# A graph network in one kernel: the attention stage's run masks computed earlier, some of its steps on GpSimd, and its block work in another place

## What is computed

```python
h = x @ W
alpha = x_i @ wa[:c] + edge_attr @ wa[c:c + ce] + x_j @ wa[c + ce:]   # x_i = h[dst], x_j = h[src]
alpha = jnp.where(alpha > 0, alpha, NEG_SLOPE * alpha)
m = jax.ops.segment_max(alpha, dst, num_segments=n)
a = jnp.exp(alpha - m[dst])
s = jax.ops.segment_sum(a, dst, num_segments=n)
out = jax.ops.segment_sum(a[:, None] * x_j, dst, num_segments=n) / (s + 1e-16) + bias
```

## Time and profile before

| | |
|---|---|
| median of 3 runs | 3713.82 us (3712.94 to 3720.65) |
| the profiled execution | 3718.32 us, of which the core's span is 3716.5 us |
| busy over the span | PE 80%, DVE 79%, ACT 59%, POOL 38% |
| mean granted clock of TensorE | 0.929 |
| dense passes | about 1353 to 1840 us |
| edge layer | about 1840 to 2796 us |
| attention stage | about 2796 to 3716 us |

### The profile page before, as it was taken

How to read it: one execution, slowest core, us unless ns; L and a number is a source line. 1 busy time by engine, 2 the same in 40 slices (tenths; PEclk the granted TensorE clock), 3 DMA queues, 4 the chain that set the end, 5 groups by cost and what they waited for, 6 DMA issues and landing times.

```text
span 3716.5 us, 122116 instructions
## 1 busy us (share of the span) xinstructions
PE 2983.3 (80%) x50473; PEld 2682.6 (72%) x50473; DVE 2931.3 (79%) x4854; ACT 2185.8 (59%) x5807; POOL 1425.5 (38%) x1155
## 2 busy tenths in 40 slices
PE   0299999999999969999777877887776878887886
PEld 0177777777777759888777777877766877777775
DVE  7599999999999933323488888888857988999996
ACT  6333333333443330000298988898866888898887
POOL 2000000000000000000089988998983555565554
PEclk9989999999999989999899999999986898899887
DMA  8156666766766679898687877777847888888784
GB/s 221 57 154 208 211 215 211 217 211 213 218 216 215 215 279 370 340 346 324 222 299 263 271 239 255 265 258 252 271 148 262 280 271 263 279 278 271 266 280 133
DMA packets 606666, 907.43 MB, mean 244 GB/s; under 512 B 358505, under 2 KB 494858, under 8 KB 587163
## 3 DMA queue, kind: packets, MB, share of 16 engines
q1 hardware_dynamic: 583992, 800.62, 66.2%
q10 hardware_dynamic: 19763, 94.38, 6.8%
q0 software_dynamic: 2352, 4.52, 0.5%
HBM read 651.96 MB, written 247.40 MB: 242 GB/s over the span
## 4 chain that ended last, share of the span: by engine, by line
PE 35%; DVE 25%; ACT 16%; issue 9%; POOL 6%; DMA 6%; ACTq 2%; DVEq 0%; SPq 0%; POOLq 0%
PE ps L648 9%; PE ps L1013 7%; ACT U L1593 4%; DMA U<-AD 4%; PE ps L673 3%; ACT U L550 3%; POOL EDG L1234 3%; DVE U L800 3%; DVE EDG L1721 2%; DVE U L1773 2%; POOL EDG L1226 2%; ACT U L1295 2%; PE ps L660 2%; PE ps L633 2%; PE ps L630 2%
## 5 line engine op out<-in xcount | busy, mean ns | idle before, releaser
L550 ACT ACTIVATE U<-ps 128x512 bf16<-128x512 f32 (+1 forms) x637 | 345.5, 571 | 460.4 <-PE ps L660 454.1
L493 POOL DMA_INDIRECT U<-REC,nod x49 | 78.4, 1600 | 1096.6 <-PE ps L604 975.6
L1226 POOL TENSOR_TENSOR EDG<-U,edge 128x512 f32<-128x512 f32 (+1 forms) x196 | 213.1, 1092 | 730.9 <-DVE edge L1378 697.7
L1593 ACT ACTIVATE U<-U,T 128x65 f32<-128x65 f32 x1806 | 459.7, 340 | 31.4 <-PE ps L1684 28.6
L1013 PE MATMUL ps<-U 128*128 128x192 bf16 x4802 | 417.9, 247 | 31.8 <-DMA U<-AD 31.2
L1013 PEld LDWEIGHTS ps<-U 128*128 128x128 bf16 x4802 | 401.8, 98 | 41.4 <-DMA U<-AD 38.4
L820 DVE TENSOR_TENSOR EDG<-edge,EDG 128x1792 bf16<-128x1792 bf16 x343 | 371.6, 1084 | 46.3 <-issue 25.9
L673 PE MATMUL ps<-EDG,U 128*128 128x193 bf16 x2401 | 313.0, 254 | 88.3 <-ACT U L550 65.8
L1621 POOL TENSOR_TENSOR U<-U 128x455 f32<-128x455 f32 x258 | 285.8, 1109 | 233.2 <-DVE U L1773 233.2
L648 PE MATMUL ps<-U 128*128 128x98 bf16 (+1 forms) x5292 | 373.2, 234 | 0.0
L648 PEld LDWEIGHTS ps<-U 128*128 128x128 bf16 x5292 | 361.8, 104 | 5.4
(11 more groups left out here) (321 smaller groups left out, 6929.6 us busy)
## 6 DMA issues: line engine op xcount, KB each, us to landing
U<-ROWS SPq DMA_DIRECT2D x411, 448.0 KB, 4.6
U<-AD SPq DMA_DIRECT2D x98, 1568.0 KB, 8.7
OND<-EDG SPq DMA_DIRECT2D x343, 224.0 KB
OSD<-EDG SPq DMA_DIRECT2D x343, 224.0 KB
AD<-U ACTq DMA_DIRECT2D x49, 1568.0 KB
EDG<-ROWS SPq DMA_DIRECT2D x171, 448.0 KB, 6.2
U<-OND SPq DMA_DIRECT2D x303, 224.0 KB, 5.0
U<-OSD SPq DMA_DIRECT2D x213, 224.0 KB, 4.7
```

The costliest lines, as they stand in the source:

```text
L550: ev4.by(act.activation(prow[i % NPW][:, P * g:P * (g + m)], ps[4 + gg % 2][:, 0:P * m], ACT.Copy))
L1226: ins = pool.tensor_tensor(VD[:, v:v + w, 0, KA * D:G * D].rearrange("p w (k f) -> p w k f", f=D), W_, bc(c_.unsqueeze(3), [P, w, G - KA, ...
L1593: ins = act.activation(V4[k % NV][:, 0, c, :], H[k % NHR][:, c, :], ACT.Copy, scale=a4[d % 2][:, s:s + 1])
```

## The change

Three things change, all for the attention stage.

1. The run masks of all 49 blocks are computed by POOL while the dense passes run (`passes_pool`), seven blocks at a time, from one load of the target numbers (2401 pieces of 256 bytes). SP stores them to memory (MSK, bf16, in seven transfers during the second pass), and in the attention stage loads 49 x 512 bytes for each block (`run_masks`) into two small buffers. PE's transpose L1641, ACT's copy L1579 and POOL's four instructions are gone there.
2. Of seven steps g = 0..6, POOL makes the values of g = 3 (`GV`) in place of ACT, with one multiplication of 128x455, and the first remainders of g = 1 and 5 (`GR`) in place of DVE. `value_at` and `rest_at` pick the semaphore to wait for. (The order on POOL: value, first remainder, second remainder.)
3. On PE the block matmuls of offsets 8, 10 and 12 come after the spread of their iteration instead of before it. On DVE the exponents (offset 15) come ahead of the first remainder.

```diff
+        def passes_pool(pool):
...
+            pool.wait_ge(msk_ld.at, msk_ld.o + 16)
+            for g in range(NGB):
...
+                msk_d.by(pool.tensor_tensor(mdif[:, :, 1:P], mdst[:, bl, 1:P], mdst[:, bl, 0:P - 1], ALU.subtract))
+                pool.wait_ge(msk_d.at, msk_d.o + 4 * g + 3)
+                msk_d.by(pool.tensor_scalar(mdif, mdif, 0.0, 1.0, ALU.is_equal, ALU.subtract))
+                pool.wait_ge(msk_d.at, msk_d.o + 4 * g + 4)
+                msk_ok.by(pool.tensor_scalar(mboth[:, bl, 0, :], mdif[:, :, 0:P], BIG, None, ALU.mult))
+                msk_ok.by(pool.tensor_scalar(mboth[:, bl, 1, :], mdif[:, :, 1:P + 1], -1.0, None, ALU.mult))
+            pool.wait_ge(msk_st.at, msk_st.o + 16 * NGB)
+
         def passes_sp(sp):
+            msk_ld.by(sp.dma_start(mdst, ROWS3[1].rearrange("d (s r) -> s d r", r=P)), 16)
             for p in range(2):
                 for i in range(NB):
                     r = i % NA
+                    if p and i % GB == GB - 1:
+                        g = i // GB
+                        sp.wait_ge(msk_ok.at, msk_ok.o + 2 * g + 2)
+                        msk_st.by(sp.dma_start(MSK[GB * g:GB * g + GB].rearrange("d s m r -> s d (m r)"),
...
             sp.wait_ge(row_mm.at, 2 * NB)
+            sp.wait_ge(msk_st.at, msk_st.o + 16 * NGB)
...
+        GV, GR = (3,), (1, 5)
...
+            def run_masks(d):
+
+                if d >= 2:
+                    sp.wait_ge(ytr.at, ytr.o + d - 1)
+                mk_ld[d % 2].by(sp.dma_start(masks[d % 2], MSK[d]), 16)
+
             sp.wait_ge(att.at, NGB)
             nt = 0
+            run_masks(0)
+            run_masks(1)
...
                 d, g, k = due4(t, 16)
-                if k is not None:
+                if k is not None and g not in GV:
                     act.wait_ge(exo.at, exo.o + d + 1)
...
+                d, g, k = due4(t, 16)
+                if k is not None and g in GV:
+                    pool.wait_ge(exo.at, exo.o + d + 1)
+                    pool.wait_ge(zok.at, zok.o + d + 1)
+                    pool.wait_ge(hev.at, hev.o + k + 1)
+                    if k >= NV:
+                        pool.wait_ge(sprd.at, sprd.o + k - NV + 1)
+                    vop.by(pool.tensor_tensor(V4[k % NV][:, 0, :, :], H[k % NHR],
+                                              bc(a4[d % 2][:, G * g:G * g + G].unsqueeze(2), [P, G, 65]), ALU.mult))
+                d, g, k = due4(t, 17)
+                if k is not None and g in GR:
+                    value_at(pool, k)
+                    rop.by(pool.tensor_tensor(V4[k % NV][:, 1, :, :], V4[k % NV][:, 0, :, :], S4[k % NV][:, 0, :, :], ALU.subtract))
                 d, g, k = due4(t, 18)
                 if k is not None:
-                    pool.wait_ge(rok.at, rok.o + k + 1)
+                    rest_at(pool, k)
...
                 d, g, k = due4(t, 17)
-                if k is not None:
-                    dve.wait_ge(vok.at, vok.o + k + 1)
+                if k is not None and g not in GR:
+                    value_at(dve, k)
...
-                    dve.wait_ge(flg.at, flg.o + 2 * d + 2)
-                    dvf.by(dve.tensor_tensor_scan(ysc, negs, ps[2][0:NB, 0:P], -BIG, ALU.add, ALU.max))
+                    dve.wait_ge(mk_ld[d % 2].at, mk_ld[d % 2].o + 16 * (d // 2 + 1))
+                    dvf.by(dve.tensor_tensor_scan(ysc, masks[d % 2][:, 0, :], ps[2][0:NB, 0:P], -BIG, ALU.add, ALU.max))
```

More of the change, by code:

```diff
@@ L1462, in cell @@
             return rows[k // 2 % n][:, e:e + P]
-        seg, negs, lastf, ylast = (Tflat[0:NB, 1225 + 130 * n:1225 + 130 * n + w] for n, w in enumerate((129, P, P, P)))
+        ylast = Tflat[0:NB, 1615:1615 + P]
+        masks = [MISC[0:NB, 1365 + P * i:1365 + P * i + P].bitcast(BF16).rearrange("p (m r) -> p m r", m=2) for i in range(2)]
+        identh = ident[0:NB, 0:NB].bitcast(BF16).rearrange("p (r h) -> p r h", h=2)[:, :, 1]
         ysc = ps[3][0:NB, P:2 * P]
@@ L1499, in due4, with value_at, rest_at @@
             return (k // G, k % G, k) if 0 <= k < NT else (None, None, None)
+        GV, GR = (3,), (1, 5)
+        def value_at(eng, k):
+            d, g = k // G, k % G
+            if g in GV:
+                eng.wait_ge(vop.at, vop.o + d * len(GV) + GV.index(g) + 1)
+            else:
+                eng.wait_ge(vok.at, vok.o + d * (G - len(GV)) + sum(h not in GV for h in range(g + 1)))
+        def rest_at(eng, k):
+            d, g = k // G, k % G
+            if g in GR:
+                eng.wait_ge(rop.at, rop.o + d * len(GR) + GR.index(g) + 1)
+            else:
+                eng.wait_ge(rok.at, rok.o + d * (G - len(GR)) + sum(h not in GR for h in range(g + 1)))
         def block4(t, off):
@@ L1544, in pairs4_sp @@
                     hots(k)
+                d = block4(t, 2)
+                if d is not None and d >= 2:
+                    run_masks(d)
                 d = block4(t, 40)
@@ L1686, in pairs4_pe @@
                     sprd.by(ins)
+                d = block4(t, 8)
+                if d is not None:
+                    pe.wait_ge(zok.at, zok.o + d + 1)
+                    if d:
+                        pe.wait_ge(ylok.at, ylok.o + d)
+                    ztr.by(pe.transpose(ps[2][0:NB, 0:P], z4[d % 2], ident[:, :]))
+                d = block4(t, 10)
+                if d is not None:
+                    pe.wait_ge(ylok.at, ylok.o + d + 1)
+                    if d:
+                        pe.wait_ge(ysok.at, ysok.o + d)
+                    pe.transpose(ps[3][:, 0:NB], ylast, ident[0:NB, 0:NB])
+                    ytr.by(pe.matmul(ps[3][:, 64:64 + NB], masks[d % 2][:, 1, :], identh, start=True, stop=True))
+                d = block4(t, 12)
+                if d is not None:
+                    pe.wait_ge(ysok.at, ysok.o + d + 1)
+                    if d:
+                        pe.wait_ge(miok.at, miok.o + d)
+                    for s in range(NB):
+                        k = G * d + s // G
+                        if s % G == 0:
+                            pe.wait_ge(od_ld[k % 4].at, od_ld[k % 4].o + 16 * (k // 4 + 1))
+                        ins = pe.matmul(ps[4][:, 4 * s:4 * s + 4], ODn[k % NOD][:, s % G, :], Y4[:, s, :], start=True, stop=True)
+                    ymm.by(ins)
         def pairs4_dve(dve):
@@ L1828, in pairs4_dve @@
                     miok.by(dve.tensor_tensor(RIf[:, d, 5:6], rest, RI[:, d, 4:5], ALU.subtract))
-                d = block4(t, 15)
-                if d is not None:
-                    dve.wait_ge(alg.at, alg.o + d + 1)
-                    dvf.by(dve.tensor_reduce(g4, ps[5][:, 0:6 * NB].rearrange("p (i v s) -> p i v s", v=2, s=3), AX, ALU.add))
-                    own()
-                    dvf.by(dve.tensor_tensor(w4, z4[d % 2], g4[:, :, 0], ALU.add))
-                    own()
-                    dvf.by(dve.scalar_tensor_tensor(w4, w4, 0.2, w4, ALU.mult, ALU.max))
-                    own()
-                    exi.by(dve.tensor_tensor(a4[d % 2], w4, g4[:, :, 1], ALU.subtract))
                 d = block4(t, 26)
@@ L2397, in _ @@
             with pool.Else():
+                passes_pool(pool)
                 pairs3_pool(pool)
```

85 lines of the change are left out of this document (28 added, 57 removed).

## The result

The changed kernel takes 3726.56 us (median of 14 runs) against 3712.03 us before (median of 14). The ratio is 1.0037, with a 95% interval from 1.0026 to 1.0048: slower by 0.4%, on the other side of the forecast of 3673 us and outside its range.

The account below looks back on a forecast made before the run. VectorE, partly kept out by GpSimd, was taken as the bound: 12.5 own work, 2.5 standing, 0.6 gaps and 1.1 to 1.3 waits a block, 45 us less over 49 blocks, plus 4 in the dense passes: 3673 us, range 3615 to 3707.

Parts of the forecast that it names:

- What bounds the kernel: Attention stage: VectorE sets the pace at 17.77 us a block, 2.3 of it standing behind GpSimd at a shared SBUF port.
- Standing behind GpSimd: Attention stage: VectorE's time kept out by GpSimd instructions, 2.3 us a block before, taken as 2.5 after.
- The wait term: VectorE in the attention stage: waits of 1.1 to 1.3 us a block, beside 0.6 us of gaps.
- bursts: GpSimd running value and remainders back to back, 3.8 and 2.8 us a block, with VectorE perhaps stalled to each one's middle.
- Block work later: TensorE in the attention stage: the spread no longer stands behind the scan, which had 75.2 us of waits.
- The cross-check: Time VectorE or GpSimd may use what they share: 15.9 us a block (89.5%) before, 15.45 (92% of 16.84) after.
- The port rival: VectorE and GpSimd's shared port stays the bound in the attention stage: block 17.26 us, 3693 us in all; chance 0.17.
- The slower rival: VectorE meets both GpSimd runs in their middle, standing 4.3 us a block instead of 2.3: 3752 us; chance 0.11.
- signs of being right: Scans 16.8 us apart, no 2.77 us L1721, its mean 0.85 to 0.95, no exp wait over 20, first AD 3 to 4 later.
- signs of being wrong: VectorE remainders at 1.5 us, index-load waits beyond 40 us, unchanged VectorE plus GpSimd time and period, or TensorE waiting for AD throughout.
- Dense passes: Start of the first pass: the new load delays the first AD block by 3 to 4 us, not given back; stores cost nothing.
- Index loads: Attention stage: shorter iterations make each tight load up to 1 us later, 24 us back, 3697 us; chance 0.10.

Follow-up runs that it names:

- off_chain: `masks_later` plus three GpSimd subtractions of 128x425 a block that wait for nobody and nobody waits for; 3750.95 us (1.0104).
- off_chain_write: `off_chain` with two fills, which read nothing, in place of each subtraction; 3691.62 us (0.9934).
- masks_later: The changed kernel without any value or first remainder on GpSimd: early masks and later block work only; 3686.19 us (0.9917 to the kernel before).
- second_first: The changed kernel with GpSimd issuing its second remainder ahead of the value and first remainder in an iteration; 3713.63 us (0.9991).
- steps_short: The changed kernel with GpSimd's value and first remainders computed for one of 65 columns, all waits and order kept; 3674.98 us (0.9879).
- later_only: The kernel before with only the new places of the block work on PE and VectorE; 3704.02 us (0.9966).
- later_all: `masks_later` with TensorE's matmuls of offset 14 behind the spread too; 3673.08 us (0.9887).

## Why the prediction was wrong

**What bounds the kernel: right.** VectorE together with GpSimd. The exclusion read in the earlier trace rows is what decided, as `off_chain` against `off_chain_write` showed. The block came out 0.9 us longer than the 16.84 forecast, and two terms of the sum share that about equally.

**Standing behind GpSimd: the step that failed.** I kept the 2.3 us of a block at 2.5 because "GpSimd's busy share stays the same". The three groups do add up to 2.3 us: L1766 3.5 x 0.25, L1761 3.5 x 0.18, the remainders 5 x 0.16. But this is the net of two changes that I didn't price apart. Without the steps, in `masks_later`, VectorE is busy 742.1 of 825 us, 15.18 us a block; with them, after 1.26 us of own work have gone, 724.1/830 x 17.74 = 15.48. So the steps brought 15.48 - (15.18 - 1.26) = 1.56 us of standing, more than the work they took, while the other two parts had brought VectorE's busy time down by 16.05 - 15.18 = 0.87. Against the sum of the forecast, 12.5 + 2.5 = 15.0 us, the changed kernel is 0.5 over; a part of this stands in small instructions with two inputs in SBUF (L1841 at 485 ns, where it was 240), which I hadn't counted; it came when the masks left, and why isn't settled.

**The wait term: failed too.** I had waits and gaps at 1.7 to 1.9 us a block; measured are (830 - 724.1)/46.8 = 2.26 us. I priced ScalarE's relief as a smaller wait, saw the first remainders in front of second ones only as bursts, and let the 1.26 us taken from VectorE shorten the block in full. ScalarE, with its shorter work, waits 150 us (111.1 and 39.2 with V in MISC) instead of 38.5 (26.7 and 11.8) for buffers V to come free, and its values come no earlier to VectorE. A part of that is GpSimd's: its second remainder is late, the spread waits for it, and 13 us went with `second_first`. But the waits alone aren't the loss. In `steps_short` VectorE is not busy for 2.54 us of a block, longer than in the changed kernel (2.30), and it is the fastest kernel with the steps. There 0.9 of the 1.26 us became waiting, while in the changed kernel 1.5 us of standing came on top.

**Block work later: the mechanism right, the place half.** Alone it gave 11 us (`later_only`) and 16 after the masks; the two can't be told apart. The forecast that the spread "no longer stands behind the scan" held, but offset 14 stayed in front of it and took over the wait: 75.6 us. Moving that too was worth another 13 us without the steps.

**The cross-check.** 6.0 + 9.45 = 15.45 us of a 17.74 us block is 87%, below the 89.5% of before. That the share of the pair would rise to 92% had no row behind it. The port rival, 3693 us, was nearest in kind, but it too took the masks' 2.3 us as worth as much as the steps' 2.8. They weren't: the narrow masks cost 12 + 4 = 16 us over 49 blocks, 0.33 us a block for 2.3 us of work, and the wide steps 0.8 us a block for 2.8 us. By the blocks of the two profiles the masks cost 0.54 us (17.77 to 17.23). Why they were so cheap isn't settled. When they left, VectorE's busy time fell by 1.0 us of a block, though the small sum of offset 7 rose from 240 to 475 ns (0.3 us a block), and its waits rose by 0.5, among them that for index loads, from 12.2 to 50.5 us in the stage.

**The slower rival.** I put it at 3752 with a chance of 0.11, by stalls in both bursts. The sign was right, the mechanism was not. It had VectorE stand until a burst ends, 1.9 and 1.4 us; measured, no comparison or first remainder took more than 1.46 us, so none stood longer than 0.8. The standing came to some 2.7 to 2.8 us (the 2.3 of the groups and 0.4 to 0.5 in small instructions), under the 3.6 from which this rival counted a loss. The kernel got slower because the waits grew as well.

**The signs.** Of the five signs of being right, four came: no 2.77 us stall, a mean of 0.93 us for the target comparison, 6.7 us of exp's wait, and the first AD rows 3.8 us later. Only the distance of the scans failed, 17.74 us and not 16.8. So the four said nothing about the time. Of the signs of being wrong the port's came, as read above.

**Dense passes: the delay right, the rest open.** 3 to 4 us were forecast, and the first block came 3.8 us later. Whether that was given back can't be told: from SP's first AD load to TensorE's last row of the passes it took 468.5 us before and 473.1 in `later_only`, both without the new load, and 475.3 in the changed kernel. In the 160 us of the second pass the stores cost nothing to be seen (152.87 us of TensorE in both).

**Index loads: not here.** 10.3 us in the changed kernel, as the block stayed long. They rise as the block gets shorter: 33.9 us in `later_all`.

## What to carry to other kernels

When two engines exclude each other, price what a move adds to the pair, and not what it adds to either: here a value taken from a third engine with room was all cost (0.57 us for each 0.945 us instruction), and a remainder moved inside the pair, that takes half as long again on the other side (0.945 us, not 0.63), was a loss too (0.17 us each). Don't count work taken from the busiest engine in full: of 1.26 us a block only 0.24 reached the block, even with next to no standing added. Price parts of opposite sign apart, even if their sum on an engine is zero. When a wait is moved from in front of an urgent instruction, list what else still stands there; the next wait in the row takes its place.

## What was not expected of the hardware

A pure fill on GpSimd left VectorE nearly alone (5 us, within noise, for 152.8 us of fills in the stage), while a subtraction of the same reach cost 65 us for 139.5. The Trainium skill states this in SBUF — State Buffer, section "Who interferes with whom": a VectorE instruction with two SBUF inputs contends with a GpSimd instruction that reads SBUF, and not with one that only writes. The trace agrees for the remainders, 701 ns beside the fills against 702 without. For VectorE's modes that use both port pairs, the same section of the Trainium skill states the contention without that exception. No run shows in which mode the comparison runs; its mean rose from 727 to 779 ns beside the fills, which would fit such a mode, weakly.

The time from the launch to the dense passes varied by 18 us between the profiled executions with the same code ahead of it, more than the effect under study, and the two profiled executions alone (3714.92 and 3718.32 us) would have shown the changed kernel as faster.
